# Message stage of a graph kernel: two PSUM banks in turn for the contractions, and the work behind them spread over the parts

## What is computed

```python
x1 = x_nodes[src].reshape(-1, N_SEG, EXTENT)          # 16 segments of 32
x2 = x_edges.reshape(-1, N_SEG, EXTENT)
i1, i2, i3 = (path_indices[:, 0], path_indices[:, 1], path_indices[:, 2])   # 64 paths
contrib = path_coeffs[None, :, None] * x1[:, i1, :] * x2[:, i2, :]
edge_out = zeros.at[:, i3, :].add(contrib)
out = zeros.at[dst].add(edge_out)                     # edges are sorted by dst
...
x = x + gnn(layernorm(x), edge_attr_512, ...)
x = x + ffn(layernorm(x)[None], ...)[0]
```

## Time and profile before

| | |
|---|---|
| median of 3 runs | 1120.15 us (1119.8 to 1122.91) |
| the profiled execution, first to last instruction | 1129.7 us (no other time of it is given) |
| its excess over the median of the runs | 9.5 us, 0.8% |
| message stage, first product to last contraction | 44.4 to 496.3 us |
| expert stage, about | 557 to 1107 us |
| busy: TensorE, VectorE, ScalarE, GpSimd | 917.5, 562.6, 227.2, 345.8 us |

### The profile page before, as it was taken

The page is one execution under the profiler, slowest core; times in us unless marked ns, Lnnn a source line. Parts: engine busy times, 40 slices in busy tenths (PEclk is TensorE's granted clock), DMA queues, the critical chain, the costliest instruction groups (busy, mean ns, idle before and its releaser), DMA issues.

```text
span 1129.7 us, 20307 instructions
## 1 busy us (share of the span) xinstructions
PE 917.5 (81%) x7194; PEld 497.2 (44%) x7195; DVE 562.6 (50%) x1321; ACT 227.2 (20%) x579; POOL 345.8 (31%) x390
## 2 busy tenths in 40 slices
PE   0156775777757767769999999999997999999988
PEld 0023333334333333337645454454543645446355
DVE  5368889889798898977621111112111111111116
ACT  1021321313222123114111111112111121121110
POOL 3715243252342534001232323223232232332220
PEclk9978898987899899999999999999998999999999
DMA  8835465464644655557699999999999999999918
GB/s 244 288 128 187 164 202 196 148 220 161 218 159 143 224 192 180 187 189 255 239 385 390 389 395 391 394 393 392 394 391 395 390 390 393 395 386 396 399 67 320
DMA packets 70341, 321.04 MB, mean 284 GB/s; under 512 B 12879, under 2 KB 13032, under 8 KB 48315
## 3 DMA queue, kind: packets, MB, share of 16 engines
q1 hardware_dynamic: 48021, 260.82, 60.7%
q0 software_dynamic: 21248, 56.55, 15.4%
q10 hardware_dynamic: 934, 1.80, 0.6%
HBM read 308.55 MB, written 13.62 MB: 285 GB/s over the span
## 4 chain that ended last, share of the span: by engine, by line
PE 64%; DVE 10%; issue 8%; another core or an unknown queue 7%; DVEq 5%; ACT 2%; DMA 0%
PE ps L1222 20%; PE ps L1268 10%; PE ps L615 8%; DVE big L596 7%; PE ps L848 6%; PE ps L1166 4%; PE ps L666 3%; PE ps L875 3%; PE ps L650 2%; DVEq L587 2%; DVEq L594 2%; PE ps L1215 2%; PE ps L1242 1%; PE ps L634 1%
## 5 line engine op out<-in xcount | busy, mean ns | idle before, releaser
L596 DVE TENSOR_TENSOR big<-big 128x512 f32 (+1 forms) x640 | 384.7, 679 | 80.4 <-remote 37.9
L615 PE MATMUL ps<-big,mixed 128*32 128x256 f32 x2512 | 181.3, 416 | 92.0 <-issue 48.2
L1222 PE MATMUL ps<-big 128*64 128x512 f32 x1024 | 240.0, 612 | 14.2 <-issue 14.2
L333 POOL DMA_INDIRECT big<-xn_d,idx x157 | 166.0, 1057 | 268.4 <-DVE big L596 207.8
L1127 POOL DMA_INDIRECT big<-h_d,idx x64 | 63.0, 984 | 359.8 <-issue 276.7
L615 PEld LDWEIGHTS ps<-big,mixed 128*32 128x32 f32 x2512 | 82.9, 118 | 184.6 <-issue 86.3
L1232 DVE TENSOR_TENSOR mixed<-big,ps 128x256 f32<-128x256 f32 x64 | 27.0, 421 | 271.1 <-ACT big L1229 270.7
L1222 PEld LDWEIGHTS ps<-big 128*64 128x64 f32 x1024 | 69.3, 139 | 139.7 <-issue 134.0
L1268 PE MATMUL ps<-big,mixed 128*64 128x256 f32 x1024 | 124.6, 385 | 0.1
L1183 POOL DMA_INDIRECT y_d<-big,sia x74 | 75.3, 1017 | 123.4 <-DVE big L1281 73.7
L625 ACT ACTIVATE mixed<-ps 128x512 f32<-128x512 f32 x40 | 23.9, 597 | 319.1 <-PE ps L615 264.8
(11 more groups left out here) (212 smaller groups left out, 673.1 us busy)
## 6 DMA issues: line engine op xcount, KB each, us to landing
big<-in_L_ffn_Wg SPq DMA_DIRECT2D x64, 1024.0 KB
big<-in_L_ffn_Wu SPq DMA_DIRECT2D x64, 1024.0 KB
big<-in_L_ffn_Wd SPq DMA_DIRECT2D x64, 1024.0 KB
big<-in_edge_attr SPq DMA_DIRECT2D x39, 1024.0 KB
big<-y_d SPq DMA_DIRECT2D x10, 768.0 KB, 12.1
big<-xn_d,idx POOLq DMA_INDIRECT x157
big<-in_L_ffn_sWg SPq DMA_DIRECT2D x2, 1024.0 KB, 5.0
big<-in_L_ffn_sWu SPq DMA_DIRECT2D x2, 1024.0 KB, 7.1
```

Source lines behind the costliest of these rows:

```text
L333: pool.indirect_dma_start(xs[s][:, c, :], None, xn_d[:, :], bass.IndirectOffsetOnAxis(ap=table[:, c0 + c:c0 + c + 1], axis=0)).then_inc(x_ ...
L596: ins = dve.tensor_tensor(pr[k % 2][:, 0:chunks, EXT * p:EXT * (p + 1)], xs[s][:, 0:chunks, ds(o1, EXT)], es[s][:, 0:chunks, ds(o2, EXT)], ...
L615: ins = pe.matmul(bank(BA)[WIN * h:WIN * (h + 1), h0:h0 + HP * EXT], onehot[s][:, CW * h + r, :], pr[k % 2][:, CW * h + r, :], start=r == ...
L1222: ins = pe.matmul(bank(k2)[TA * h:TA * (h + 1), :].rearrange("p (w f) -> p w f", w=2), xgT[k2][:, k, 0:TA], gu[:, :, k, W * h:W * (h + 1)] ...
```

## The change

Two PSUM banks, 0 and 1, take the contractions of even and odd pairs. The bank BT_ for turned data is gone: a pair is turned into its own bank once that has been copied out. A contraction that begins a pair waits for `evt_ok` of the pair two before, which used the same bank, in place of `ev_ok` of the last one. The loop runs over the 8 parts: turn and evict_turned of the last pair stand behind the contraction of an even part, its selection behind that of the odd part that follows. The puts of the last group go one by one behind parts 2 to 6, the one-hot rows of the next group in groups of four behind parts 2 to 5, `place_rows` behind part 7, and `evict_sums` behind part 1 of the next group. The further rounds add their sums at their own end, inside the condition, and the waits behind them become constants.

```diff
@@ -555,18 +555,25 @@
     put_ok = sem("put_ok")
     more_ok, idxx_ok, added_ok = sem("more_ok"), sem("idxx_ok"), sem("added_ok")
     regs = [[dve.alloc_register(f"off{k}_{m}") for m in range(2 * HP)] for k in (0, 1)]
-    BA, BT_, BS, BM = 0, 1, 2, 3
+    BA, BS, BM = 0, 2, 3
+
+    def edge_bank(qq):
+
+        return bank(BA + qq % 2)
+
     def at(t, *of):
         return isinstance(t, int) and t in of
-    def one_hots(t, s, bias, chunks=EC):
-
-        if not at(t, 0, 1):
+    def one_hots(t, s, bias, c0=0, c1=EC, chunks=EC):
+
+        if c0 == 0 and not at(t, 0, 1):
             act.wait_ge(part_used, SUB * t - SUB)
-        for c in range(chunks):
+        for c in range(c0, min(c1, chunks)):
             ins = act.activation(onehot[s][:, c, :], iotaw[:, 0:WIN], ACT.Abs, bias=bias(c))
+        if c1 < chunks:
+            return
         ins.then_inc(oh_ab, 1)
         act.wait_ge(oh_ab, t + 1)
         act.activation(onehot[s][:, 0:chunks, :], onehot[s][:, 0:chunks, :], ACT.Relu, scale=-1.0,
@@ -606,14 +613,14 @@
         pe.wait_ge(part_ok, SUB * t + k + 1)
         if k == 0:
             pe.wait_ge(oh_ok, t + 1)
-        if k % 2 == 0 and (k > 0 or not at(t, 0)):
-            pe.wait_ge(ev_ok, PARTS * t + k // 2)
+        if k % 2 == 0 and (k > 2 or not at(t, 0)):
+            pe.wait_ge(evt_ok, PARTS * t + k // 2 - 1)
         for r in range(CW):
             for h in range(QW):
                 if CW * h + r >= chunks:
                     continue
-                ins = pe.matmul(bank(BA)[WIN * h:WIN * (h + 1), h0:h0 + HP * EXT], onehot[s][:, CW * h + r, :],
-                                pr[k % 2][:, CW * h + r, :], start=r == 0,
+                ins = pe.matmul(edge_bank(k // 2)[WIN * h:WIN * (h + 1), h0:h0 + HP * EXT],
+                                onehot[s][:, CW * h + r, :], pr[k % 2][:, CW * h + r, :], start=r == 0,
                                 stop=r == min(CW, chunks - CW * h) - 1)
         ins.then_inc(part_used, 1)
@@ -623,15 +630,13 @@
         if qq > 0 or not at(t, 0):
             act.wait_ge(tp_ok, PARTS * t + qq)
         act.activation(ev.rearrange("p (u q) -> p u q", q=PP),
-                       bank(BA).rearrange("p (q u) -> p u q", q=PP), ACT.Copy).then_inc(ev_ok, 1)
+                       edge_bank(qq).rearrange("p (q u) -> p u q", q=PP), ACT.Copy).then_inc(ev_ok, 1)
     def turn(t, qq):
         pe.wait_ge(ev_ok, PARTS * t + qq + 1)
-        if qq > 0 or not at(t, 0):
-            pe.wait_ge(evt_ok, PARTS * t + qq)
         for f in range(FPP):
-            ins = pe.transpose(bank(BT_)[:, P * f:P * (f + 1)], ev[:, P * f:P * (f + 1)], ident[:, :])
+            ins = pe.transpose(edge_bank(qq)[:, P * f:P * (f + 1)], ev[:, P * f:P * (f + 1)], ident[:, :])
         ins.then_inc(tp_ok, 1)
     def evict_turned(t, qq):
@@ -639,7 +644,7 @@
         act.wait_ge(tp_ok, PARTS * t + qq + 1)
         if qq > 0 or not at(t, 0):
             act.wait_ge(sel_ok, PARTS * t + qq)
-        act.activation(evT, bank(BT_), ACT.Copy).then_inc(evt_ok, 1)
+        act.activation(evT, edge_bank(qq), ACT.Copy).then_inc(evt_ok, 1)
     def select(t, qq):
@@ -673,7 +678,7 @@
     after(act, V, v_win)
     after(act, G, g_const)
-    one_hots(0, 0, lambda c: wdst[:, c:c + 1], EC0)
+    one_hots(0, 0, lambda c: wdst[:, c:c + 1], chunks=EC0)
     rows_stored(dve)
     dve.wait_ge(s_fill, n_fill)
     after(dve, V, v_sel)
@@ -685,20 +690,29 @@
             gather_sources(1 - s, idx, EC * (t + 1), SUB * t)
         chunks = EC if t else EC0
         products(t, s, 16 * QW * (t // 2 + 1), 16 * EC * (t // 2) + 16 * (EC if s else EC0), chunks)
-        for qq in range(PARTS):
-            contract(t, s, 2 * qq, chunks)
-            contract(t, s, 2 * qq + 1, chunks)
-            evict(t, qq)
-            turn(t, qq)
-            evict_turned(t, qq)
-            select(t, qq)
-            if t > 0 and qq < 2:
-                put(t - 1, range(3) if qq == 0 else range(3, NB), start=t == 1)
-            if qq == 1 and t + 1 < NG:
-                one_hots(t + 1, 1 - s, lambda c: wdst[:, EC * (t + 1) + c:EC * (t + 1) + c + 1])
-            if qq == 2:
+        for k in range(SUB):
+            contract(t, s, k, chunks)
+            q = PARTS * t + k // 2 - 1
+            if q >= 0 and k % 2 == 0:
+                turn(q // PARTS, q % PARTS)
+                evict_turned(q // PARTS, q % PARTS)
+            if q >= 0 and k % 2 == 1:
+                select(q // PARTS, q % PARTS)
+            if k % 2 == 1:
+                evict(t, k // 2)
+            if t > 0 and k == 1:
+                evict_sums(t - 1)
+            if t > 0 and 2 <= k < 2 + NB:
+                put(t - 1, range(k - 2, k - 1), start=t == 1)
+            if t + 1 < NG and 2 <= k < 6:
+                one_hots(t + 1, 1 - s, lambda c: wdst[:, EC * (t + 1) + c:EC * (t + 1) + c + 1],
+                         CW * (k - 2), CW * (k - 1))
+            if k == SUB - 1:
                 place_rows(t, nrow[:, t:t + 1])
-        evict_sums(t)
+    turn(NG - 1, PARTS - 1)
+    evict_turned(NG - 1, PARTS - 1)
+    select(NG - 1, PARTS - 1)
+    evict_sums(NG - 1)
     put(NG - 1, range(NB), stop=True)
     gu_in = [sem(f"gu_in{k}") for k in range(4)]
@@ -743,17 +757,14 @@
         pool.wait_ge(idxx_ok, x + 1)
         pool_ready()
         gather_sources(1, idxx, 0, chunks=chunks)
-        dve.wait_ge(put_ok, NB * t)
-        dve.wait_ge(added_ok, NB * x + 1)
-        for b in range(NB):
-            add_block(b).then_inc(added_ok, 1)
+        dve.wait_ge(added_ok, NB * x + NB + 1)
         dve.tensor_scalar(wdx[:, :], wdst[:, ds(c0, EC)], woff[:, ds(j + 1, 1)], None, ALU.add)
         dve.tensor_scalar(nrx[:, :], nrow[:, ds(g, 1)], woff[:, ds(j + 1, 1)], None, ALU.subtract
                           ).then_inc(more_ok, 1)
         products(t, 1, 16 * QW * (NG // 2 + x + 1),
                  16 * EC * (NG // 2) + 16 * EC0 + j * (16 * EC0 + 16 * EC * (NG - 1)) + 16 * EC * g, chunks)
         act.wait_ge(more_ok, x + 1)
-        one_hots(t, 1, lambda c: wdx[:, c:c + 1], chunks)
+        one_hots(t, 1, lambda c: wdx[:, c:c + 1], chunks=chunks)
         place_rows(t, nrx[:, :])
         for qq in range(PARTS):
             contract(t, 1, 2 * qq, chunks)
@@ -765,8 +776,15 @@
         evict_sums(t)
         pe.wait_ge(added_ok, NB * x + NB + 1)
         put(t, range(NB), start=True, stop=True)
-
+        dve.wait_ge(put_ok, NB * t + NB)
+        for b in range(NB):
+            add_block(b).then_inc(added_ok, 1)
+
+    none_left = sem("none_left")
     with nc.If(nmax > 0):
+        dve.wait_ge(put_ok, NB * NG)
+        for b in range(NB):
+            add_block(b).then_inc(added_ok, 1)
         with nc.Fori(0, nmax) as j:
             sync.wait_ge(part_ok, SUB * (j * NG + NG))
             more_item(j, 0, 0, EC0)
@@ -774,8 +792,10 @@
                 first = sync.value_load(gtab[0:1, ds(g, 1)], min_val=0, max_val=NE_EDGES - GE)
                 sync.wait_ge(part_ok, SUB * (j * NG + g + NG))
                 more_item(j, g, first, EC)
-
-    nput = nmax * (NG * NB) + NG * NB
+        for b in range(NB):
+            dve.memset(bank(BM + b), 0.0).then_inc(none_left, 1)
+        dve.wait_ge(none_left, NB)
+
     nparts = nmax * (NG * SUB) + NG * SUB
     y_out = [sem(f"y_out{s}") for s in range(4)]
@@ -791,9 +811,7 @@
     load_expert(2, 2)
     def add_messages(b):
-        dve.wait_ge(put_ok, nput - (NB - 1 - b))
-        if b == 0:
-            dve.wait_ge(added_ok, nput - (NG * NB - 1))
+        dve.wait_ge(put_ok, NB * (NG - 1) + b + 1)
         VV(add_block(b))
     ln2 = layer_norm(lambda b: H[:, b, :], add_messages)
...
```

4 lines of the change are left out of this document (2 added, 2 removed).

## The result

| | before | after |
|---|---|---|
| median of the timed runs | 1121.53 us (1119.80 to 1126.93, 4 runs) | 1079.65 us (1079.29 to 1080.32, 4 runs) |
| the profiled execution, its span | 1129.7 us | 1078.3 us |
| mean granted TensorE clock, of full speed | 0.949 | 0.970 |
| message stage, first product to last product | 44.36 to 494.28 us | 43.28 to 444.44 us |

The change makes the kernel faster: 41.9 us less, ratio 0.963 with a 95% interval of 0.9597 to 0.9662. The forecast was 1091 us, with a range of 1076 to 1114. The sign and the range held, and the gain was 42 us where 29 were forecast.

What follows compares the result with a forecast made beforehand. VectorE was taken to bound the message stage, DMA the expert stage. Terms: 31.9 + 4.7 - 4.0 - 0.9 = 31.7 us less when profiled, taken as 29 for timed runs: 1120.15 - 29 = 1091 us, range 1076 to 1114.

Steps and rivals of the forecast that it cites:

- What bounds the kernel.: VectorE bounds the message stage wherever nothing holds it, 39.1 us a group; DMA bounds the expert stage, which shifts whole.
- Stalls before parts 4, 6 and 0: 31.9 us go: Message stage: all 31.9 us of these VectorE stalls vanish, as long as a contraction takes under 4.9 us.
- Stalls before part 2: Message stage: 1.9 us stays in each of 8 groups with gathers, 15.2 us; 4.7 of 19.9 us go.
- New lateness: Contractions 2 to 4 start sooner and meet landing data: 0.5 us a group lost, 4.0 us in all.
- End of the stage: After the last group's products, place_rows and the third pair's selection precede the last turned eviction: 0.9 us lost, once.
- The scale from the profile to the runs: Profiled span is 9.5 us over the median; gain of 31.7 us, or 27 at 85%, taken as 29 us.
- Rival A: Message stage: contraction 0 is late because TensorE was behind, so all stalls go: 51 us less, 1069 us; chance 0.08.
- Rival B: Contractions 2 and 3 meet landing data as contraction 0 does: gain only 6 us, up to 1114 us; chance 0.14.
- Rival D: TensorE becomes the message stage's bound in strict order: slower, 24 us more at 4.6 us a contraction, 1144 us; chance 0.05.
- Rival E: Evenly spread work holds TensorE at 1.2 GHz in the message stage: 60 us more, 1180 us; chance 0.04.
- Rival C: Late contractions belong mostly to the profiled execution; timed runs gain only 1 to 3 us, 1118 us; chance 0.09.

Runs made afterwards that it cites:

- the best version: Changed kernel with group 1's gathers released two per part of group 0 and place_rows behind part 6, against the changed kernel: 1066.78 us, ratio 0.9494.

## Why the prediction was right or wrong

*What bounds the kernel.* Right. VectorE sets the pace of the message stage; with its stalls gone it is 385.0 us busy of a stage of 401. The expert stage moved as a whole.

*"Stalls before parts 4, 6 and 0: 31.9 us go".* Right. None is left in the changed kernel, and the cause is the one named: selection and puts in front of contraction 2, on top of late contractions. The two runs that separate order and banks show that it is the order alone.

*"Stalls before part 2", 15.2 of 19.9 us stay.* This is the step that failed. 17.3 went and 2.6 stayed. I took contraction 0 to be slow by landing data, 6.4 us whatever stands around it, because groups 1, 3 and 6 had started it in time and still lost 1.8 to 1.9 us. It took 5.0 us in the changed kernel, 0.1 more than VectorE's room. So this is not a fixed length of work, but the moment at which a signal gets through. In group 1 GpSimd's first six gathers end at 98.12 us and the next begin at 99.38; the semaphore rises between them, at 99.20. In the profile of before, contraction 0 began at 95.31, 0.2 us later against its gathers; they paused from 99.07 to 100.34, and the semaphore rose at 101.75, inside the next three.

The traces bear this out as a pattern. The five traces of the new order with all gathers on chip A have 40 contractions 0 in groups 1 to 8. Of these, 33 took 4.98 to 5.12 us, and the semaphore rose 0.1 to 0.25 us before the next gather began; the other 7 took 5.75 to 5.81 us, and it rose 0.6 us after that beginning; none lies between. The first cost VectorE 0.2 to 0.4 us, the others 1.1. In the old order the contractions 0 that started in time took 4.9, 5.6 or 6.4 us, again with nothing between. That the changed kernel's own trace, and its second one, have only the short kind is in part luck: the run with one bank has three of the long kind, the one-hot rows in one piece two, the best version two. That a signal has to wait for a pause is still not shown: of the 31 late signals in the changed kernel's groups 1 to 8, 24 rise in a pause and 7 while a gather is being issued.

*"New lateness", 4.0 us.* None came. Contractions 2 and 3 do meet the gathers, as forecast, and take 3.7 to 4.5 us, near to the 4.2 us of the row that it rested on. But TensorE has only 1.5 to 2.0 us of other work beside them in a part, and the room of 4.9 us holds. I had charged for a backlog after part 0 that a contraction of 5.0 us hardly leaves.

*"End of the stage", 0.9 us.* Right in kind: 0.6 us by the place of `place_rows`, as the later runs show, plus 0.95 for the clock of one execution.

*The scale from the profile to the runs.* The step was right and worth its place. The terms as measured on the profiled executions are 31.9 + 17.3 - 0 - 1.6 = 47.6 us (the spans differ by 51.4), and the medians differ by 41.9. That the profiled execution of before has stalls that typical ones lack is borne out by the old order's second trace, 41.0 us of stalls against 51.8. With 85% of the stalls, the share that the prediction worked out, the gain is 44 - 2.6 - 1.6 = 40 us. So nearly the whole miss of 13 us is two terms: part 2, from which 17.3 us went in place of 4.7, and the new lateness, 0 in place of 4.0. Both were off the same way, so they did not cancel; it was the width of the range that held the result.

*Rival A* (all stalls go, 1069 us) was closest in what happened, but its price was not scaled; with the 85% it would have been 1077. Its reason, contraction 0 late because TensorE was behind, was wrong: contraction 0 is still late with TensorE in time.

*Rival B* fell: contractions meet the gathers and lose nothing. *Rival D* fell for the size: its point was 4.1 us for parts 0 to 5, measured are 5.0, 4.6, 4.5, 4.4, 2.0, 2.0, mean 3.75; and its sum charged every part in strict order, where the late signal of one step does not hold up the start of the next. Contraction 1 starts at 99.17, when contraction 0's signal has not come. It also counted 1.8 us of other work in every part, as if each had a put; with five puts in eight parts its own rows give 1.5. *Rival E* fell: the granted clock rose from 0.949 to 0.970. The Trainium skill's case of PSUM cycling ("TensorE: Matmul & The Clock Gate", section "A second HAM failure mode: psum-queue depth-cycling") has no counterpart here: the granted clock does drop to its lower level for 3.4 us about once a group, but cycling two banks and using one gave nearly the same mean, 0.970 and 0.972.

*Rival C* (nothing to win outside the profile, a 9% chance) fell on chip A, whose timed runs show the whole gain. On chip B it may be the truth. The three timed kernels there, all in the new order, have ratios of 0.997 to 0.9995. They differ from the changed kernel only in when transfers are released, and have no late signal, and the kernel before itself takes 57 us less than on chip A, about what its stalls of group 0 and after come to (13.2 + 41 to 52 us). That it has no stalls there is suggested by this, but not shown: neither it nor the changed kernel was traced on chip B, and the changed kernel was not timed there either. So the gain of 4% is shown for one chip only.

**What stays open.** How gathers delay TensorE's signals and, in group 0, the issue of its matmuls; whether their bytes or their instructions do it; and why one chip shows it and another, at the same pace of gathers and transfers, did not. That the gathers cause it on chip A is shown, by taking them away in both orders and by spreading them in group 0.

## What to carry to other kernels

When a wait is put down to "remote", compare the modelled end of the work with the time at which the waiting engine starts, stage by stage, and look at what the engine does next. If that starts on time and is signalled right behind the late signal, it is the signals that are late rather than the work, and late signals ask for room, not for speed. In a pipeline in which one engine sets the pace, spread what another engine does behind each step so that every step has the pacing engine's whole period for its longest work; here, on a chip with late signals, that was worth 38 us of the stage, and a further buffer almost nothing. Release gathers two at a time beside work rather than all ahead of it, and time a change on more than one chip before its size is believed.

## What was not expected of the hardware

- On chip A, while GpSimd issues gathers back to back (0.95 us each, 0.30 apart), the semaphore of a 1.98 us contraction rises 3.7 to 5.1 us after its start in the changed kernel, and up to 7.7 us in the kernel before; with one gather or none per part, at 1.98 us, or up to 3.7 at the lower clock, as long as its records. The turn behind it is signalled 0.06 us after it, 2.04 us after the end of its records (107.00, 109.04).
- With 29 gathers in a row, until 61 us, contractions 0 and 1 of group 0 took 17.2 and 13.7 us, and TensorE's own records show gaps of 1.5 to 2.4 us between single matmuls. The last of these gaps ends at 64.64 us, 3.4 us after the last gather was issued.
- Transfers by SyncE alone delayed nothing: without gathers, at 4 MB of edges per group, every contraction's signal came 0.05 us after the end of its own records (1.93 us at the full clock).
- Another chip ran the kernel before in 1065.25 us in place of 1122.7; four variants of the changed kernel traced there show no such delay.
- The granted clock rose with the change, 0.949 to 0.970 over the span and 0.92 to 0.96 in group 8. It is not the even spread as such: the old order without most gathers has 0.977.
